# Splitting layer 1's expert weights during layer 0, moving the routed products to VectorE, and spreading the first ratio row with TensorE

## Time and profile before

| | us |
|---|---|
| median of 3 runs | 1051.53 |
| profiled execution | 1050.06 |
| its span | 1048.2 |
| PE busy (TensorE matmuls) | 1010.6, 96% |
| DVE busy (VectorE) | 524.3, 50% |
| POOL busy (GpSimd) | 354.5, 34% |
| ACT busy (ScalarE) | 314.4, 30% |
| mean traffic | 130 GB/s |

### The profile page before, as it was taken

One profiled execution on the slowest core, in us unless ns is written; L12 is line 12 of the kernel. 1 busy time (PEld: TensorE's weight loads), 2 busy tenths in 40 slices (PEclk: granted clock), 3 DMA queues, 4 the chain that ended last, 5 costly groups with the idle time before them and its releaser, 6 DMA issues.

```text
span 1048.2 us, 14852 instructions
## 1 busy us (share of the span) xinstructions
PE 1010.6 (96%) x4893; PEld 837.2 (80%) x4895; DVE 524.3 (50%) x886; ACT 314.4 (30%) x550; POOL 354.5 (34%) x351
## 2 busy tenths in 40 slices
PE   8899999999999999999999999999989999999993
PEld 5678887888888887888867777778778999999992
DVE  3788777455565455555566333665543314443000
ACT  3743332211121112111242010301144545454541
POOL 4123245410000000000042000022168889898873
PEclk9999999999999999999999999999999999999997
DMA  7387543443433434453444101005155665665433
GB/s 239 130 297 272 161 136 122 166 161 114 140 123 121 153 128 161 142 181 123 138 159 151 41 1 41 1 1 198 58 187 108 163 163 142 141 146 119 80 61 40
DMA packets 51322, 136.41 MB, mean 130 GB/s; under 512 B 8708, under 2 KB 10004, under 8 KB 50772
## 3 DMA queue, kind: packets, MB, share of 16 engines
q1 hardware_dynamic: 36660, 108.15, 30.1%
q0 software_dynamic: 12432, 25.71, 12.4%
q10 hardware_dynamic: 2192, 2.08, 0.7%
HBM read 96.85 MB, written 39.07 MB: 130 GB/s over the span
## 4 chain that ended last, share of the span: by engine, by line
PE 85%; DVE 4%; POOL 4%; DMA 2%; issue 1%; ACT 1%; ACTq 1%; PEldq 0%; POOLq 0%; PEld 0%; DVEq 0%
PE ps_y L1687 6%; PE ps_y L1689 6%; PE ps_y L1688 5%; PE ps_h L1645 5%; PE ps_h L1647 5%; PE ps_h L1646 5%; PE ps_u L1700 3%; PE ps_u L1699 3%; PE ps_h L1933 2%; PE ps_y L1933 2%; PE ps_y L1928 2%; PE ps_y L1929 2%; PE ps_y L1856 2%; PE ps_y L1857 2%; PE ps_h L1840 2%; PE ps_h L1841 2%
## 5 line engine op out<-in xcount | busy, mean ns | idle before, releaser
L1202 DVE TENSOR_TENSOR h<-h,wb 128x512 f32<-128x512 f32 x64 | 44.4, 693 | 162.6 <-ACT h L903 162.5
L897 ACT ACTIVATE h<-ps_h,bias 128x512 f32<-128x512 f32 x64 | 44.0, 689 | 235.1 <-PE ps_h L1654 235.1
L685 POOL DMA_DIRECT2D s_raw<-in_sgu x8 | 4.3, 544 | 299.9 <-DVE g_lo L1210 192.1
L1687 PE MATMUL ps_y<-w_hi,g_hi 128*128 (+1 forms) x256 | 102.2, 399 | 3.5 <-DVE g_lo L1210 3.5
L1689 PE MATMUL ps_y<-w_hi,g_lo 128*128 (+1 forms) x256 | 101.2, 395 | 0.0
L1688 PE MATMUL ps_y<-w_lo,g_hi 128*128 (+1 forms) x256 | 101.0, 395 | 0.0
L1645 PE MATMUL ps_h<-xt_hi,w_hl 128*128 128x512 f32 x256 | 100.0, 391 | 0.7 <-ACT lg_t L846 0.7
L1647 PE MATMUL ps_h<-xt_hi,w_hl 128*128 128x512 f32 x256 | 100.3, 392 | 0.0
L1646 PE MATMUL ps_h<-xt_lo,w_hl 128*128 128x512 f32 x256 | 100.2, 391 | 0.0
L1477 DVE CAST eg_hi<-e_raw 128x704 fp32r<-128x704 f32 x32 | 16.7, 581 | 138.0 <-PE ps_y L1958 125.3
L903 ACT ACTIVATE h<-ps_h,bias 128x512 f32<-128x512 f32 x64 | 43.9, 688 | 115.4 <-PE ps_h L1667 115.4
(11 more groups left out here) (319 smaller groups left out, 2455.5 us busy)
## 6 DMA issues: line engine op xcount, KB each, us to landing
w_hl<-w1s_d SPq DMA_DIRECT2D x49, 704.0 KB, 4.1
w1s_d<-w_hl SPq DMA_DIRECT2D x16, 704.0 KB, 5.9
e_raw<-in_wgu SPq DMA_DIRECT2D x8, 1408.0 KB, 7.1
w_raw<-in_w1b SPq DMA_DIRECT2D x16, 608.0 KB, 4.7
xres<-in_x SPq DMA_DIRECT2D x16, 256.0 KB, 4.5
acc<-x_d SPq DMA_DIRECT2D x4, 1024.0 KB, 7.6
xc_d<-xc SPq DMA_DIRECT2D x4, 1024.0 KB, 4.8
e_raw<-in_wdn SPq DMA_DIRECT2D x8, 512.0 KB, 8.4
```

Source lines behind the costliest of these rows:

```text
L1202: tt(h1[u][:], h1[u][:], wb[:, v, :], ALU.mult).then_inc(gch, 1)
L1687: mm(ps_y[:, j, :], g_hi[u][:, cols], sl(w2_hi), start=first, **kw)
```

## The change

Three parts, and one small move.

1. The weights of experts 1 to 7 are laid out by the host in 42 units of 128 x 768 (`we1`; 6 per expert). In layer 0, from super-tile 1 on, each step of 64 handles one unit k: GpSimd's queue loads it, ScalarE rounds it (`high_unit`) after the step's gelus, VectorE subtracts (`low_unit`) after the step's `hidden_tile`, and GpSimd's queue stores both halves in `e_d`. There are two unit buffers; a load waits for the stores of the unit two before. The loads start behind the cond loads in GpSimd's list. In layer 1 `split_expert` remains for expert 0 alone, and SyncE loads finished halves (`load_halves`), once the buffer is free.
2. In layer 1's slot tiles `x_low`, `products` and `g_low` move from GpSimd to VectorE and read PSUM directly. ScalarE's three unrounded copies (L1005, L1016, L1023) go. `scatter_add(t)` is no longer one tile behind.
3. The first row of ratios is spread by TensorE: VectorE widens it into `zf[1]`, four small matmuls with the identity put it over all partitions, ScalarE copies it to `wb`. The store to `wrow_d` stays, behind it; the load L882 goes.
4. At the start both `second` are issued ahead of `router_and_u1(3)`, not in its middle.

```diff
@@ memory and buffers
+    UNITS, UW = 6, we1.shape[2] // 6
+    AHEAD = UNITS * (E - 1)
+    e_d = scr("e_d", (E - 1, 2, P, UNITS * UW))
+        pre_hi = [sb_ahead(f"pre_hi{u}", [P, UW], F32R)[:] for u in range(2)]
+        pre_raw = [sb_ahead("pre_raw0", [P, UW])[:], u1t[:, 0:UW]]
@@ SyncE, layer 1
+            def load_halves(e):
+                b, gu = e % 2, DC * 2 * H1
+                for k, (eg, ed) in enumerate(((eg_hi, ed_hi), (eg_lo, ed_lo))):
+                    sp.dma_start(eg[:, b].rearrange("p c n -> p (c n)").bitcast(F32),
+                                 e_d[e - 1, k, :, 0:gu]).then_inc(half_in, 16)
+                    sp.dma_start(ed[:, b].rearrange("p c n -> p (c n)").bitcast(F32),
+                                 e_d[e - 1, k, :, gu:gu + HC * D]).then_inc(half_in, 16)
-            for s in range(NS):
+            for s in range(NS - 1):
                 store_acc(s)
+            for u in range(2):
+                sp.wait_ge(pre_st[u], 32 * (AHEAD // 2))
+            sp.wait_ge(gu_done, NS * SH)
+            load_halves(1)
+            store_acc(NS - 1)
             for e in range(1, E):
-                load_expert(e)
+                if e >= 2:
+                    tiles = sp.value_load(last_tile[0:1, e:e + 1], min_val=0, max_val=SLOT_TILES)
+                    sp.wait_ge(ry_done, 1 + tiles)
+                    load_halves(e)
+                sp.wait_ge(half_in, 64 * e)
+                sp.wait_ge(e_done, e)
+                sp.sem_inc(e_done, 1)
@@ GpSimd, layer 0
                 for h in range(2):
                     load_matrix(pool, cw1, 1, SEQ, cw1_in[h], j, h)
+            pool.wait_ge(w1_lo_done, 2 + FT)
+            pool.wait_ge(w2_lo_done, FT)
+            pool.wait_ge(z_ok, 4)
+
+            def load_unit(k):
+                u = k % 2
+                if k >= 2:
+                    pool.wait_ge(pre_st[u], 32 * (k // 2))
+                at = k % UNITS * UW
+                pool.dma_start(pre_raw[u], we1[k // UNITS, :, at:at + UW]).then_inc(pre_in[u], 16)
+
+            def store_unit(k):
+                u = k % 2
+                pool.wait_ge(pre_lo_done, k + 1)
+                at = k % UNITS * UW
+                for n, src in enumerate((pre_hi[u].bitcast(F32), pre_raw[u])):
+                    pool.dma_start(e_d[k // UNITS, n, :, at:at + UW], src).then_inc(pre_st[u], 16)
+
+            load_unit(0)
+            load_unit(1)
+            for k in range(AHEAD):
+                store_unit(k)
+                if k + 2 < AHEAD:
+                    load_unit(k + 2)
             pool.wait_ge(g_done, 2 + (NS - 1) * FT)
@@ GpSimd, layer 1
             for t in range(SLOT_TILES):
-                g_low(t)
-                if t + 1 < SLOT_TILES:
-                    products(t + 1)
-                if t + 2 < SLOT_TILES:
-                    x_low(t + 2)
                 if t + 5 < SLOT_TILES:
                     gather(t + 5)
-                if t:
-                    scatter_add(t - 1)
-            scatter_add(SLOT_TILES - 1)
+                scatter_add(t)
@@ ScalarE
+            masks(0)
+            act.wait_ge(rho_all, 1)
+            nc.scalar.copy(wb[:, 0, :], ps_y[:, 2, :]).then_inc(wb_in[0], 16)
             rho_rows(0)
...
-            act.dma_start(wb[:, 0, :], wrow_d[0:TPS, :].rearrange("(o j) p -> o (j p)", o=1).partition_broadcast(P))\
-                .then_inc(wb_in[0], 16)
+            def high_unit(k):
+                act.wait_ge(pre_in[k % 2], 16 * (k // 2 + 1))
+                nc.scalar.copy(pre_hi[k % 2], pre_raw[k % 2]).then_inc(pre_hi_done, 1)
             for s in range(1, NS):
                 for f in range(FT):
                     if s == 1 and f == 1:
                         rho_rows(1)
                     gelus(s * FT + f, f, f % 2, s - 1 if f == 1 else None)
+                    if (s - 1) * FT + f < AHEAD:
+                        high_unit((s - 1) * FT + f)
                     if s + 1 < NS and f == 1:
                         masks(s + 1)
@@ VectorE
+            dve.wait_ge(w01_ok, 1)
+            nc.vector.tensor_copy(zf[1][:].rearrange("p (j n) -> p j n", n=P),
+                                  rho[:, 0:TPS].unsqueeze(2).to_broadcast([P, TPS, P])).then_inc(rho_wide, 1)
             low_w2(0)
             low_w2(1)
             logits(2)
             place_z(0)
+            dve.wait_ge(rho_all, 1)
             place_z(1)
+            def low_unit(k, u):
+                dve.wait_ge(pre_hi_done, k + 1)
+                tt(pre_raw[u].bitcast(F32R), pre_raw[u], pre_hi[u].bitcast(F32), ALU.subtract).then_inc(pre_lo_done, 1)
                     hidden_tile(s * FT, v, 0, sums=s - 1)
+                    low_unit((s - 1) * FT, 0)
                     add_moved(s - 1)
                     hidden_tile(s * FT + 1, v, 1)
+                    low_unit((s - 1) * FT + 1, 1)
...
-            for e in range(1, E):
-                dve.wait_ge(e_in, 48 * (e + 1))
...
+            def x_low(t):
+                dve.wait_ge(xg_hi_done, t + 1)
+                tt(xg_lo[:].rearrange("p c n -> p (c n)"), ps_u[:, 0, :],
+                   xg_hi[:].rearrange("p c n -> p (c n)").bitcast(F32), ALU.subtract).then_inc(xg_lo_done, 1)
...
@@ TensorE
+            def rho_over_rows():
+                pe.wait_ge(rho_wide, 1)
+                for j in range(TPS):
+                    last = mm(ps_y[:, 2, j * P:(j + 1) * P], zf[1][:, j * P:(j + 1) * P], ident[:],
+                              start=True, stop=True)
+                last.then_inc(rho_all, 1)
             masks(0)
+            rho_over_rows()
             logit_rows(2)
...
-            router_and_u1(3, between=seconds)
+            seconds()
+            router_and_u1(3)
```

More of the change, by code:

```diff
@@ L339, in adaln_ffn @@
         out_st = sem("out_st")
+        pre_in = [sem(f"pre_in{u}") for u in range(2)]
+        pre_hi_done = sem("pre_hi_done")
+        pre_lo_done = sem("pre_lo_done")
+        pre_st = [sem(f"pre_st{u}") for u in range(2)]
+        half_in = sem("half_in")
         e_in = sem("e_in")
@@ L1036, in copies @@
                     silu(t + 1, 1 - u)
-                g_high(t, first=stored is None and n == 0)
-                if nxt:
-                    up(t + 1, 1 - u)
+                g_high(t)
                 if nxt2:
@@ L1042, in copies @@
                 weigh(t, n, stored)
-            x_high(0, first=True)
+            x_high(0)
             silu(0, 0, first=True)
-            up(0, 0)
             x_high(1)
@@ L1231, in low_s @@
                     dve.wait_ge(z_done, 2 + STEPS)
+                else:
+                    for u in range(2):
+                        dve.wait_ge(pre_st[u], 32 * (AHEAD // 2))
                 hi, lo, raw = shared_halves(n)
@@ L1544, in _, with products, g_low, slot_tile @@
                             split_expert(0, 0, k)
-            for e in range(1, E):
-                dve.wait_ge(e_in, 48 * (e + 1))
-                if e >= 2:
-                    tiles = dve.value_load(last_tile[0:1, e:e + 1], min_val=0, max_val=SLOT_TILES)
-                    dve.wait_ge(ry_done, 1 + tiles)
-                for k in range(4):
-                    split_expert(e, e % 2, k)
+            def x_low(t):
+                dve.wait_ge(xg_hi_done, t + 1)
+                tt(xg_lo[:].rearrange("p c n -> p (c n)"), ps_u[:, 0, :],
+                   xg_hi[:].rearrange("p c n -> p (c n)").bitcast(F32), ALU.subtract).then_inc(xg_lo_done, 1)
+            def products(t, u, first=False):
+                dve.wait_ge(rs_done, t + 1)
+                dve.wait_ge(rup_done, t + 1)
+                if not first:
+                    dve.wait_ge(rgt_done, t)
+                tt(rg[:, 0:H1], rs[:], ps_y[:, u, 0:H1], ALU.mult).then_inc(rg_done, 1)
+            def g_low(t):
+                dve.wait_ge(rgt_hi_done, t + 1)
+                tt(rgt_lo[:].rearrange("p c n -> p (c n)"), ps_u[:, 1, 0:HC * P],
+                   rgt_hi[:].rearrange("p c n -> p (c n)").bitcast(F32), ALU.subtract).then_inc(rgt_lo_done, 1)
+            def slot_tile(t, u, nxt=True, nxt2=True):
+                g_low(t)
+                if nxt:
+                    products(t + 1, 1 - u)
+                if nxt2:
+                    x_low(t + 2)
+            x_low(0)
+            products(0, 0, first=True)
+            x_low(1)
+            for t in range(2):
+                slot_tile(t, t)
+            with dve.Fori(1, (SLOT_TILES - 2) // 2) as m:
+                for u in range(2):
+                    slot_tile(m * 2 + u, u)
+            for t in range((SLOT_TILES - 2) // 2 * 2, SLOT_TILES):
+                slot_tile(t, t % 2, t + 1 < SLOT_TILES, t + 2 < SLOT_TILES)
         @block.tensor
```

68 lines of the change are left out of this document (23 added, 45 removed).

## The result

The changed kernel takes **1108.11 us** (median of 4 runs, 1103.3 to 1109.14); the kernel before, beside it on the same chip, 1051.82. The ratio is **1.053, 95% interval 1.0507 to 1.0559**. I had predicted 1087, with 1098 as the upper end: the sign was right, the size fell outside the range. The profiled execution took 1109.14 us, 59.1 more than the one that my sum was made against.

What follows compares the result with a forecast made beforehand. Only what TensorE waits for, and its tail, was taken to count. Terms +45.7 + 1.7 + 0.5 - 0.7 - 3.0 - 3.2 - 4.5 = +36.5 on 1050.06 gave 1086.6, stated as 1087 us; range 1079 to 1098.

Steps and rivals of the forecast that it cites:

- The stall: Super-tile 1: ScalarE waits for the first unit's load, queued behind the cond loads, and TensorE goes on late: +45.7 us.
- The start: First row of ratios comes early from TensorE, but VectorE's widening copy stands ahead of place_z: -0.7 us (-2.3 to +1).
- The clock: After the long stall TensorE runs for 3.3 us at granted clock 0.50: +1.7 us, bounds 0 and 5.
- The other 41 units ... no cost: Layer 0: roundings and subtractions fit the step, and GpSimd's queue takes 6.4 of 7.39 us, stores landing in 4.8.
- Rival (a): Layer 0: GpSimd's queue becomes the bound if the two stores land in more than 5.8 us; chance 0.11, mostly mild form.
- its mild form: Layer 0: stores land in 6.3 us, costing 0.5 on each of 40 units: +20 us, 1107.
- its strong form: Layer 0: stores land in 7.6 us, 1.8 more on some 40 units less 3 us of buffer slack: +69, 1155.
- The masks: Super-tiles 1 and 2: next masks are copied behind a unit's rounding, 0.85 later each, delaying TensorE: +0.5 us (0 to 1.7).
- The slot tiles: Layer 1: work moved to VectorE removes waits for gather, gates, rgt_lo and xg_lo, and slow clock: -3.0 and -3.2 us.
- gather, gates and clock: Slot tiles' start: tile 2's gather wait 2.0, first two tiles' gates 1.0 and slow clock 1.6 us go away.
- The tail: End of kernel: the last tiles' adds are issued at once, 5.8 us apart, ending at 1035.0 instead of 1039.5: -4.5 us.
- Rival (b), halves late: Layer 1: experts' 4352 KB halves arrive some 2 us late at each of three short experts: 1092 to 1094; chance 0.10.

Runs made afterwards that it cites:

- Experiment 1: Changed kernel with the 64 cond loads issued from SyncE's steps of super-tile 1 instead of GpSimd's list: 1060.73 us, ratio 1.0065.
- experiment 9: Kernel with one store per unit (low halves not stored), plus SyncE storing 384 KB of other weights per unit: 1045.94 us, ratio 0.9949.
- 7: On top of Experiment 1, each half stored when ready, the next load waiting for the low half's landing alone: 1048.59 us, ratio 0.9969.
- 5: On top of Experiment 1, SyncE issues the units' loads too, so nothing in GpSimd's list waits for a landing: 1056.24 us, ratio 1.005.
- 8: As 7, but with the units' loads on SyncE's queue behind w_hl's load of the step: 1061.93 us, ratio 1.0096.
- 6: On top of Experiment 1, GpSimd issues the load of unit k+1 right behind the stores of unit k: 1082.25 us, ratio 1.0291.
- experiment 4: Kernel before with only the early row spread by TensorE and both seconds ahead of the router's product: 1052.09 us, ratio 0.9998.
- experiment 11: On top of 5, part two undone: GpSimd subtracts and multiplies for slot tiles again, adds one tile behind: 1097.09 us, ratio 1.0431.
- experiment 10: Kernel before with only the last three tiles' adds issued without the lag of one tile: 1051.61 us, ratio 0.9998.
- experiment 2: On top of Experiment 1, one store per unit: low halves not stored, layer 1 takes the rounded half instead: 1040.59 us, one run.

## Why the prediction was wrong

**The stall: right.** +44.6 for +45.0, the 45.7 of the stall and the -0.7 of the start; the loads' end, the landing (3.5 for 3.9), the rounding (0.83 for 0.85) and the hand-overs. Experiment 1 gives stall and clock together as 47.4.

**The clock: right in kind, too few cases.** At 1.2 GHz (granted 0.50) TensorE went on at 219.88:

```profile
219.00:223.00 4.00, 3.12 (x13) 2.40 (x14) 3.29 (x5) 3.83 (x9) 1.08 (x2) 0.50 0.37 143
...
548.00:554.00 6.00, 3.65 (x9) 2.88 (x10) 2.42 (x4) 2.11 (x3) 1.61 (x3) 0.50 0.60 179
```

(TensorE's busy time is the third number; the clock the one before the last two.) The stall costs about 1.6. But two of the later waits are followed by it too, at 400 and 548, for some 3.5 together, and so is the wait of 2.1 for sh_lo at 766, 1.6. Before, the same wait near 692 was followed by a clock of 1.00.

**"The other 41 units ... no cost": this step failed.** I took 4.8 us for the landing of the stores, the lower of my two bounds, from a 1024 KB store on a quiet stretch, and reasoned that 768 KB are less. The second store took 5.8 at the median of all 42 units and up to 9.3. The 4.8 would have done for super-tile 1 (3.8 at the median); in super-tiles 2 and 3 it was 6.3 and 6.9, and all eight later waits on h lie there. The sum has a slip as well: it puts the landing behind both issues, while the rows count it from the start of an issue, so its threshold of 5.8 is 6.3 in the rows' count. In the sum's own count, the idle time in front of the next load, the median is 5.7, and 16 of the 24 turns from 348 us on are above 5.8, but only one of the 16 before.

Rival (a) names this mechanism, and its mild form, 6.3 us and 1107, comes near the measured time; it had a chance of 0.11. That the number is so near is luck: it takes 0.5 us on each of 40 units, without the slack that its strong form takes off, and the time was lost in eight waits, the slow clock behind two of them and some scattered parts.

I looked at the bytes and at one mean rate, but not at when in the step a store goes out beside w_hl's load. GpSimd's own issues did not grow, 0.542 us at the median for all 84 stores; the page that the prediction weighed (the Trainium skill, "SBUF — State Buffer", section "SBUF: two separate sides") states that VectorE's fast float32 copies keep GpSimd from writing descriptors, and in the length of the issues this trace shows next to nothing of it, 0.707 at most for one store. The landings don't rule it out. Of the second stores within 1.5 us of a w_hl load, the 8 that have such a copy running in the 1.1 us from their start land in 8.05 and 7.14 us (medians of the two buffers), the 8 without one in 6.47 and 6.19. Of the cond loads of the kernel before, beside a w_hl load, the 17 with a copy land in 4.16 and 3.96 us (medians of cw and side_col), the 6 without in 1.91 and 2.15. So the prediction's reading that the trace shows 0.1 of it looked at the issues alone. No run here sets the copies and the w_hl load apart, and this rival stays open.

Two things were missing from the working as well. First, only GpSimd's turn was added up, not the round of a buffer, rounding to rounding, which has 12.8 of 14.8 us at good landings. Which of the two bound the units is not settled: experiments 7 and 9 shorten both and win 12 and 15 us; 5 takes away the turn alone and wins at most 4.5, but has some 9 us of new loss at the masks; 8 does both and wins nothing. As far as they go, they show together that the landing of the second store ahead of the next load is what cost. Second, the bytes have a price on TensorE's own loads, 5 to 6 us by experiment 9.

In the changed kernel the second stretch's +29.1 is: 19.0 of waits on h, 5.1 of clock in layer 0, 1.6 of clock at 766, and 3.4 that I did not place one by one; 2.2 of them are there without any store too, by the time of ScalarE's first xs_hi (539.25 for 537.01).

**The masks: right for what could be seen.** No wait on m_base of its own beyond 0.3 in experiment 1; but in 5, 6 and 8, with the load late, this place has the longest single wait (3.4, 8.0 and 5.4).

**The start: nothing, within the bounds.** TensorE's waits for g_lo fell from 3.5 to 1.7, and tile 16 began 0.3 later (164.38 for 164.12); in experiment 4, with the early row alone, it began at the same time.

**The slot tiles: -9.8 for -6.2.** The first weighed tile comes 13.3 us after the first xg_hi instead of 17.6, -4.3 for the -4.6 of gather, gates and clock. The other 5.5 are from the rest: from weighed tile to weighed tile it is now 6.69 to 6.84 us up to the last three, where before two early turns took 8.04 and 7.74 and about every fourth of the later ones 6.98 to 7.21. I had 1.6 for this. These are absent in experiment 11 as well (its own long turns are those beside the halves' loads), so they went with the experts' own split, not with the moved products; what in it made them I have not shown.

**The tail: right, to the tenth.** -4.5; the adds lie 5.4 us apart (for the 5.8 of my step) and the last begins 2.2 after the last tile is weighed (for 2.3):

```profile
1088.05 1.55 POOL L809 DMA_INDIRECT out_x<-yt,slot_tok  x1 [4.69 <-issue]
1093.47 1.55 POOL L809 DMA_INDIRECT out_x<-yt,slot_tok  x1 [3.87 <-ACT yt L1053]
1098.85 1.55 POOL L809 DMA_INDIRECT out_x<-yt,slot_tok  x1 [3.83 <-DMA out_x<-yt,slot_tok]
```

**Rival (b), halves late: no.** TensorE's waits show one of 0.9 at the first gate and none at a later expert. The burst of the halves meets the adds instead, and by experiment 11 the slot tiles would have taken 35 us more had part two not been made with it. The two parts belong together: without part two, the split ahead makes this stretch 25.5 us longer than in the kernel before, where with it it is 9.8 shorter; and a piece of part two without the split, the tail, gave nothing (experiment 10). The moved products alone on the kernel before were not tried.

**The chances.** "Slower" at 0.95 was right. The range was too narrow: the step with the widest pair of bounds (4.8 and 7.6) and a threshold of 5.8 between them was given as a yes.

## What to carry to other kernels

Where a new chain runs through a ring of buffers, add up its whole round (load, each engine's turn, store, landing) against the ring's depth times the step, beside each engine's or queue's own turn, and with landings from a stretch that is as crowded as it will be, at the place in the step where the transfer will go out. A wait for a landing in an in-order list holds up everything behind it: put stores that are ready ahead of it, and nothing that TensorE needs behind it. And before work is put behind another loop in a queue, read when that loop ends and when the first consumer asks: here that alone cost some 46 us, clock included.

## What was unexpected of the hardware

A store of 384 KB landed in 3.2 us where it was the only one of its step (experiment 2), and in 4.5 and 6.0 us as the first and second of a pair issued 0.54 apart (the changed kernel; medians of e_d<-pre_hi and e_d<-pre_raw, issue to landing). With the same bytes the second of the pair took 3.8 us at the median where it went out 3.2 us ahead of w_hl's 704 KB load (units 2 to 14 of the changed kernel) and 5.9 to 9.3 within 1 us of it. 65 MB of added traffic, which took the mean rate from 130 to 182 GB/s, well under the 345 seen in a stretch, moved w_hl's landing from 4.1 to 5.2 us: mean rates say little about when one transfer lands.

The clock is a large part of what short waits cost here: in experiment 11 TensorE waited 20.3 us for rgt_lo and then ran at a granted clock of 0.50 for 30.7 us, some 15 more; in experiment 1 some 8.5 us of layer 0 went the same way.
